# Local block: each transfer of a projection's parted weights divided into four by columns

## The reference, cut to what matters

```python
def attn_layer(x, Wqkv, qs, ksc, Wo):
    b, n, _ = x.shape
    qkv = x @ Wqkv                      # 128 -> 3 x 1024, six layers
    q, k, v = jnp.split(qkv, 3, -1)
    ...
    q = l2norm(q) * qs
    k = l2norm(k) * ksc
    ...
    out = local_attention(q, k, v)      # 16 heads of 64, windows of 32
    ...
    return out @ Wo
```

## Time and profile before

| | |
|---|---|
| Time of three runs | 4389.3, 4388.34, 4383.0 us; median 4388.34 us |
| Profiled execution | its own time 4397.17 us, span of the trace 4395.4 us |
| Mean granted clock of PE | 0.957 |
| Busy: PE, PEld | 4076.7 us (93%), 2997.6 us (68%) |
| Busy: DVE, POOL, ACT | 3413.3 us (78%), 2918.9 us (66%), 2584.6 us (59%) |

### The profile page before, as it was taken

The page is one execution under the profiler, slowest core; times in us unless marked ns, Lnnn a source line. Parts: engine busy times, 40 slices in busy tenths (PEclk is TensorE's granted clock), DMA queues, the critical chain, the costliest instruction groups (busy, mean ns, idle before and its releaser), DMA issues. The chain is left out here.

```text
span 4395.4 us, 151802 instructions
## 1 busy us (share of the span) xinstructions
PE 4076.7 (93%) x66856; PEld 2997.6 (68%) x66856; DVE 3413.3 (78%) x4235; ACT 2584.6 (59%) x3022; POOL 2918.9 (66%) x3425
## 2 busy tenths in 40 slices
PE   8999969999999999999968888799999999999997
PEld 5655557777787777777733333577877777787775
DVE  5636568887888897898568884788888888888884
ACT  3424436666666666667427775366666667666663
POOL 2202158888888888888524441688888888888883
PEclk8989989999999999999969998899999999999998
DMA  4304322333233232232100000323232233333221
GB/s 143 127 10 137 108 88 78 78 87 83 70 81 93 77 82 74 77 88 74 39 11 1 1 1 1 98 77 91 80 82 74 80 85 83 85 84 83 73 68 35
DMA packets 164545, 316.97 MB, mean 72 GB/s; under 512 B 38760, under 2 KB 42480, under 8 KB 156848
## 3 DMA queue, kind: packets, MB, share of 16 engines
q1 hardware_dynamic: 153520, 241.18, 20.4%
q0 software_dynamic: 10368, 66.06, 4.7%
HBM read 92.03 MB, written 20.05 MB: 25 GB/s over the span
## 5 line engine op out<-in xcount | busy, mean ns | idle before, releaser
L696 PE MATMUL psum<-loc_w_hl,loc_z_lo 128*128 128x512 f32 x1152 | 515.5, 447 | 33.5 <-DMA loc_w_hl<-parted 24.6
L1097 POOL TENSOR_TENSOR loc_prob<-loc_prob,loc_recip 128x1024 f32<-128x1024 f32 x192 | 365.9, 1906 | 179.6 <-DVE loc_recip L1219 177.8
L942 ACT ACTIVATE loc_sq<-psum 128x1024 f32<-128x1024 f32 x192 | 197.0, 1026 | 478.6 <-PE psum L698 473.6
L1079 POOL TENSOR_TENSOR loc_rc_k<-loc_rc_k,loc_rs_k 128x1024 f32<-128x1024 f32 x192 | 454.7, 2368 | 21.8 <-DVE loc_rs_k L1196 21.8
L1182 DVE TENSOR_REDUCE loc_ssq<-loc_sq 128x16 f32<-128x1024 f32 x384 | 463.9, 1208 | 4.3 <-POOL loc_rn L1075 4.3
L698 PE MATMUL psum<-loc_w_hl,loc_z_hi 128*128 128x512 f32 x1152 | 460.5, 400 | 4.6 <-issue 4.6
L697 PE MATMUL psum<-loc_w_hl,loc_z_hi 128*128 128x512 f32 x1152 | 460.2, 400 | 0.1
L1079 POOL TENSOR_TENSOR loc_rc_q<-loc_rc_q,loc_rs_q 128x1024 f32<-128x1024 f32 x192 | 460.2, 2397 | 0.0
L793 PE MATMUL psum<-loc_PT,loc_V 64*64 64x32 f32 x24576 | 409.7, 221 | 14.9 <-issue 14.4
L793 PEld LDWEIGHTS psum<-loc_PT,loc_V 64*64 64x64 f32 x24576 | 386.3, 136 | 41.0 <-issue 17.7
L813 PEld LDWEIGHTS psum<-loc_outT,loc_wo 128*128 128x128 f32 x3072 | 383.5, 197 | 24.5 <-issue 7.9
(11 more groups left out here) (198 smaller groups left out, 9803.3 us busy)
## 6 DMA issues: line engine op xcount, KB each, us to landing
loc_V<-loc_V SPq DMA_DIRECT2D x1152, 128.0 KB
loc_V<-loc_V SPq DMA_DIRECT2D x672, 64.0 KB
loc_w_hl<-parted POOLq DMA_DIRECT2D x36, 1024.0 KB, 8.0
parted<-moe_halves POOLq DMA_DIRECT2D x18, 1024.0 KB, 5.2
moe_spread<-moe_gates SPq DMA_DIRECT2D x64, 256.0 KB, 4.1
moe_raw<-in_wqkv POOLq DMA_DIRECT2D x18, 512.0 KB, 5.9
moe_w<-in_moe_w SPq DMA_DIRECT2D x32, 256.0 KB, 3.4
loc_wo<-in_wo SPq DMA_DIRECT2D x12, 512.0 KB, 3.5
```

What stands on the lines that cost most here:

```text
L696: pe.matmul(M.bank[bank + g], z_lo[:, r, tokens], w_hl[:, k, 0, cols], start=True, stop=False)
L1079: pool.tensor_tensor(rc, rc, rs[:, :], ALU.add).then_inc(added, 1)
L1097: pool.tensor_tensor(both, both, spread_heads(recip[:, :], 2 * WINDOW), ALU.mult).then_inc(p_ready, 1)
```

## The change

Each `load_parts` issues four transfers in place of one, each with 256 of the 1024 columns of both parts. They go to the same place from the same place, and PE waits for the sum of all four (64 in place of 16 on the semaphore).

```diff
-            sp.wait_ge(wk_loaded, DEPTH * 16)
-            sp.wait_ge(wq_loaded, DEPTH * 16)
-            sp.wait_ge(wv_loaded, DEPTH * 16)
+            sp.wait_ge(wk_loaded, DEPTH * 64)
+            sp.wait_ge(wq_loaded, DEPTH * 64)
+            sp.wait_ge(wv_loaded, DEPTH * 64)
...
-                    pe.wait_ge(wk_loaded, L * 16 + 16)
+                    pe.wait_ge(wk_loaded, L * 64 + 64)
...
-                    pe.wait_ge(wv_loaded, L * 16 + 16)
+                    pe.wait_ge(wv_loaded, L * 64 + 64)
...
-                    pe.wait_ge(wq_loaded, L * 16 + 16)
+                    pe.wait_ge(wq_loaded, L * 64 + 64)
...
             def load_parts(L, k, loaded):
                 slot = 3 if k == 1 and L % 2 else k
-                pool.dma_start(w_hl[:, slot, :, :], M.parted[L, :, k, :, :]).then_inc(loaded, 16)
+                for g in range(4):
+                    cols = slice(g * INNER // 4, (g + 1) * INNER // 4)
+                    pool.dma_start(w_hl[:, slot, :, cols], M.parted[L, :, k, :, cols]).then_inc(loaded, 16)
```

## The result

Over 11 runs each the changed kernel takes 4401.72 us (4390.29 to 4417.16) against 4385.01 us (4375.77 to 4394.8): ratio 1.0037, 95% interval 1.0025 to 1.0050, some 16 us slower. The profiled execution has 4406.86 us of its own, a span of 4404.9 us and a mean granted clock of 0.961; that is 9.7 us and 9.5 us above the one of before.

What follows compares the result with a forecast made beforehand. PE was taken to bound the block, with POOL close behind. Added POOL issues cost 45 us, less 15.6 for shorter gaps and 19.5 for clock: +10 us, 4398 us against the median; range 4362 to 4427.

Steps and rivals of the forecast that it cites:

- likeliest case: Whole kernel: a small loss, 4388 to 4412 us, chance 0.34.
- Issue price: POOL's time for one quarter-load issue: 0.94 us, the middle of bounds 0.65 and 1.23; a load holds POOL 3.1 us longer.
- rival 1: Faster: an issue on POOL hardly depends on rows, 0.65 us; costs 17 against 35 us of gain, 4370 us; chance 0.32.
- rival 3: An issue on POOL costs in proportion to packets, 1.23 us; +39 us, 4427 us; chance 0.08.
- decision point: An issue of about 0.83 us in the loop, where costs (about 35 us) equal gains.
- k loads: Ten loads ahead of `scaled` and turn_q: POOL's added time less 11.1 us of cover costs 20 us (8.6 to 32).
- Starts: Start of both blocks: twelve issues instead of three delay `rest_of_tokens` and PE; 8.6 us (2.8 to 14).
- Gaps: PE's "issue" idle at ten layer boundaries, 31.2 us, from late instructions behind long transfers; half, 15.6 us, given back.
- Rival 2: Boundary gaps stay, as the fetch stands behind everything queued; 29 us of cost remain, 4417 us; chance 0.18.
- Clock: Granted clock falls after boundary gaps, up to 26 us over ten; three quarters, 19.5 us, credited for halved gaps.
- q loads: Ten loads in the loop: POOL idles 7.57 us behind them, so added issues cost nothing if PE's stall leaves some.
- -19 us for the boundaries: Layer boundaries: v loads cost 16 us, q loads nothing, against 15.6 us from gaps and 19.5 us from the clock.

Runs made afterwards that it cites:

- The memset run: Against the kernel before: weight loads stay whole 1 MB transfers, with 2.22 us of memset on POOL behind each of the 36 issues; ratio 1.0194, 85 us slower.

## Why the prediction was right, and by which steps

The direction, the size and the likeliest case held: +10 us forecast, +9.5 in the trace and 16 by the medians, which is in the range given for that case. But its parts were less right than their sum, and that the sum came out is in part luck: too high a price for POOL stood against too large a return at the boundaries.

- **Issue price: too high.** 0.733 us in the median against 0.94, between the fixed price and the proportional one but near the fixed end. A load holds POOL 4 x 0.733 - 0.65 = 2.3 us longer, not 3.1. Row work exists (272 packets against 48 cost 0.23 us more), so rival 1's premise was nearly right and rival 3 is out.
- **By the prediction's own rule** this price lies below its decision point of 0.83 us. k would cost 8 x 2.3 - 11.1 + 2 x 2.3 = 11.9 us, v 10 x 2.3 - 14.9 = 8.1, the two starts 7, together 27 against 35 of gain: 8 us faster. The kernel was slower, so errors lie on the other side.
- **k loads: the reckoning was right.** 20 us were forecast at 0.94 us an issue, 11.9 follow at the measured price; the run that divides them alone is 12 us slower, and the traces with and without k divided differ by 12 us in the mean. Its waits are where they were forecast: turn_q's rose by 9.8 us in that run, turn_probs' by 1.2.
- **Starts: 8.6 forecast, 10.1 in the trace**, 1.0026 (11 us) alone. The mechanism was right, PE waits for `rest_of_tokens`: 32.0 us in two waits, where it waited 24.6 us in three for the weights. The rule of the Trainium skill that the prediction cited ("DMA: Bandwidth & Descriptors", "Rules for kernel authors") gave 12 us, an estimate, by a delay of the transfers; the wait is for POOL, and no run with pieces by columns shows such a delay.
- **Gaps: halving forecast, 31.2 to 13.2 measured** for those above 1.3 us, but 38.3 to 26.5 for all "issue" time at the boundaries: 12 us given back, not 15.6. v's division does most of it: with v divided this time is 24.6 to 28.7 us in six traces, without it 31.1 to 38.3 in six others. (The memset run, 27.9 us with whole transfers, is left out: PE waited 66 us for DVE there.) Rival 2, that the gaps stay, is refuted. That PE's own instructions stood behind the long transfer is consistent with this, but no row shows a fetch that waits; and shorter pieces by partitions, which keep 8 KB rows, did nothing (39.9 us). Whether the size of a piece or of a row decides is open.
- **Clock: 19.5 us were credited.** The time at 1.2 GHz at the boundaries fell by 34 us, from 51.2 to 17.1. A matmul took 0.63 us there instead of 0.39, so 34 us give back some 13 us, and 17 at most if half of the work is lost at half the clock; these two are estimates.
- **The step that failed: "q loads: nothing, as long as PE's stall leaves some of it", and with it -19 us for the boundaries.** At the measured price it would have been -27; they gave 7.9 us back. The 7.57 us of idle time that POOL had behind the q load was 4.5 to 7.6 us at each of the ten boundaries before and is 0.0 at nine of them after, since PE's stall is gone. So q's delay is felt: turn_q at the boundaries waits 3.0 us for POOL where it waited for nothing (0 also with v alone or q alone). turn_probs waits 8.9 us where 8.1 follow for v, and PE waits 3.6 us more for DVE. With 12 us of "issue" time less, PE's idle time at the boundaries did not fall at all, it rose from 43.3 to 46.6 us; what the boundaries gained goes with the clock.
- **The term that was missing: DVE.** The products of the tables cost 56 us in the kernel before, where 12 x 1.5 = 18 would do, and the q issue moves POOL's long reads away from them. With v divided already, q's division makes the boundaries 25 us shorter (705.3 to 680.4): PE's waits for DVE fall from 21.8 to 1.3 us and its time at 1.2 GHz from 41.0 to 13.7. By that sum the change would have been near 1.009 without it, an estimate; this was not run.

So the division has a part that pays, v with q (0.9945), and two that only cost: k 0.3% and the starts 0.3%. What stays open is how these add up. By medians the product of the parts is 0.9999 and the change has 1.0037, a difference of 0.0038 with an uncertainty of about 0.003 by the four intervals. The traces show no such difference: fills and loops less those of before are -11.6 us for v and q, +17.4 for k and +11.1 for the start, in sum +16.9, and the changed kernel has +16.7. So the ratio of v and q may be somewhat low by chance; the rows can't decide. One thing they do show: in the changed kernel the first boundary of loc0 took 76.0 us against 66.7 to 70.1 for its others, with table products of 7.05 us and PE's longest wait for DVE, 4.3 us. Why POOL and DVE meet at that boundary alone was not settled.

## What to carry to other kernels

When work is put on an engine that is nearly full, ask two things. Is the idle time that is to hide it there because of the very stall that the change removes? And whom does the work meet in its new place? Here a second engine's operations lasted three to five times as long next to POOL's long ones. Test a change to several like transfers one by one and in pairs: v and q gain nothing singly and 0.55% together, and k and the starts take that away again. When a gap is gone, add up all idle time and the time at the lower clock before calling it a gain: with v alone most of the gaps were gone and PE idled 15 us more. If an operation's mean in the grouped view is well above its shortest (1218 against 409 ns before, for one table product; the mean is 434 with v and q divided), look for what runs beside it before moving anything.

## What the runs showed of the hardware

- An issue of a DMA on POOL's software queue takes 0.52 us on average with 48 packets, 0.62 with 144 (0.53 to 0.66) and 0.75 with 272 (0.72 to 0.84); the first of a group takes 0.07 to 0.09 us more than those right behind it.
- A memset of 2520 columns on POOL, 2.22 us, held up a DVE product with a scalar on 32 columns (4.08 us; 0.2 to 2.7 us in the other kernels here).
- Four DVE products of 256 columns with both inputs in SBUF take 1.5 us beside short POOL operations or DMA issues, and up to 7 us where some of them meet POOL operations on 1024 columns; a product that is held up ends 0.28 us after the POOL operation.
- PE sat idle without a cause in the profile for up to 4.3 us behind a 1 MB transfer in 8 KB rows; with all transfers in pieces of 1 KB rows for up to 3.2 us, and at half of the boundaries for less than 1.3.
